# Neighbourhood attention block: four K window copies move from GpSimd to ScalarE

## The reference

```python
def _arsinh_norm(x, w, b):
    return w * jnp.arcsinh(x) + b
def _na2d(x, qkv_w, qkv_b, proj_w, proj_b, num_heads=8, k=3):
    qkv = x @ qkv_w + qkv_b
    q, kk, v = jnp.split(qkv, 3, axis=-1)
    ...
    nb_k = kk[:, ri, ci].reshape(B, H, W, k * k, num_heads, hd)   # the 3x3 neighbours, clipped at the edges
    nb_v = v[:, ri, ci].reshape(B, H, W, k * k, num_heads, hd)
    scores = jnp.einsum('bijnd,bijmnd->bijnm', q, nb_k)
    attn = jax.nn.softmax(scores, axis=-1)
    out = jnp.einsum('bijnm,bijmnd->bijnd', attn, nb_v).reshape(B, H, W, C)
    return out @ proj_w + proj_b
h1 = _arsinh_norm(h, n1_w, n1_b)
h = h + _na2d(h1, qkv_w, qkv_b, proj_w, proj_b)
h2 = _arsinh_norm(h, n2_w, n2_b)
ff = jax.nn.gelu(h2 @ mlp_w1 + mlp_b1, approximate=False) @ mlp_w2 + mlp_b2
return h + ff
```

## Time and profile before

| | |
|---|---|
| median of 3 runs | 4491.67 us (4490.61 to 4491.87) |
| the profiled execution | 4491.05 us, of which 4489.3 us are the span from the first to the last instruction |
| TensorE matmul, busy | 4311.2 us (96%) |
| VectorE, busy | 3710.5 us (83%) |
| ScalarE, busy | 3322.0 us (74%) |
| GpSimd, busy | 4023.6 us (90%) |
| mean granted TensorE clock | 0.991 of full |
| DMA, hardware queue | 591.32 MB, 50.6% of 16 engines |

### The profile page before, as it was taken

The page is one execution under the profiler, slowest core; times in us unless marked ns, Lnnn a source line. Parts: engine busy times, 40 slices in busy tenths (PEclk is TensorE's granted clock), DMA queues, the critical chain, the costliest instruction groups (busy, mean ns, idle before and its releaser), DMA issues.

```text
span 4489.3 us, 136686 instructions
## 1 busy us (share of the span) xinstructions
PE 4311.2 (96%) x53320; PEld 3075.6 (69%) x53320; DVE 3710.5 (83%) x7716; ACT 3322.0 (74%) x4865; POOL 4023.6 (90%) x4604
## 2 busy tenths in 40 slices
PE   3899999999999999999999999999999999999997
PEld 2577667667667667767767767766766766776775
DVE  4788888888888888888888888888888888888884
ACT  2677777777777777777777777777777777777774
POOL 1699999999999999999999999999999999999995
PEclk9899999999999999999999999999999999999998
DMA  3455555555555555555555555555555555555551
GB/s 77 127 137 140 137 136 141 138 136 141 136 136 140 136 137 136 140 138 137 138 138 138 138 139 137 138 139 135 141 136 136 141 135 137 139 138 137 138 133 50
DMA packets 593556, 600.06 MB, mean 134 GB/s; under 512 B 76559, under 2 KB 540561, under 8 KB 590353
## 3 DMA queue, kind: packets, MB, share of 16 engines
q1 hardware_dynamic: 592912, 591.32, 50.6%
HBM read 197.69 MB, written 135.40 MB: 74 GB/s over the span
## 4 chain that ended last, share of the span: by engine, by line
POOL 82%; issue 13%; PE 2%; DVE 1%; ACT 1%; SPq 1%; POOLq 0%; DMA 0%; DVEq 0%; ACTq 0%
POOL p_lo L1044 28%; POOL g_lo L1070 10%; POOL k_win L1087 10%; POOL b_hi L1059 7%; POOL a_lo L1052 6%; POOL b_lo L1061 6%; POOL g_hi L1068 6%; POOL a_hi L1050 3%; POOL k_win L1096 3%; POOL k_win L1104 2%; PE ps L378 2%; SPq L288 0%; POOLq L1042 0%; SPq L314 0%; DMA v_rows<-v_nat 0%
## 5 line engine op out<-in xcount | busy, mean ns | idle before, releaser
L1044 POOL TENSOR_TENSOR p_lo<-prob,p_hi 100x512 f16<-100x512 f32 x1024 | 1378.5, 1356 | 249.7 <-ACT p_hi L985 241.8
L984 ACT ACTIVATE prob<-ps 100x512 f32<-100x512 f32 x1024 | 612.8, 598 | 532.1 <-PE ps L378 530.6
L378 PEld LDWEIGHTS ps<-v_win,p_hi 100*128 100x128 f16 x8192 | 475.6, 98 | 247.6 <-issue 107.1
L843 DVE TENSOR_TENSOR o_norm<-ps,recip 64x128 f32<-64x128 f32 x2048 | 591.1, 289 | 49.4
L1070 POOL TENSOR_TENSOR g_lo<-g,g_hi 128x512 f16<-128x512 f32 x512 | 595.1, 1162 | 41.0
L985 ACT ACTIVATE p_hi<-ps 100x512 f16<-100x512 f32 x1024 | 616.4, 602 | 0.0
L812 DVE TENSOR_REDUCE ps<-ps 128x8 f32<-128x800 f32 x512 | 509.4, 995 | 85.0 <-PE ps L378 80.9
L378 PE MATMUL ps<-v_win,p_hi 100*128 100x65 f16 x8192 | 515.1, 193 | 60.5 <-POOL p_lo L1044 48.9
L378 PE MATMUL ps<-w_hi,g_hi 128*128 128x256 f16 x2048 | 560.7, 274 | 0.0
L378 PE MATMUL ps<-w_lo,g_hi 128*128 128x256 f16 x2048 | 560.5, 274 | 0.0
L378 PE MATMUL ps<-w_hi,g_lo 128*128 128x256 f16 x2048 | 560.5, 274 | 0.0
(11 more groups left out here) (103 smaller groups left out, 12106.9 us busy)
## 6 DMA issues: line engine op xcount, KB each, us to landing
keys<-k_win SPq DMA_DIRECT2D x1536, 100.0 KB, 2.2
v_win<-v_rows SPq DMA_DIRECT2D x1024, 101.6 KB
queries<-q_nat SPq DMA_DIRECT2D x1536, 64.0 KB
v_rows<-v_nat SPq DMA_DIRECT2D x256, 260.0 KB, 5.4
xin<-in_x_dram SPq DMA_DIRECT2D x128, 512.0 KB, 4.5
out_dram<-y SPq DMA_DIRECT2D x256, 256.0 KB, 3.1
queries<-in_query_mask_dram SPq DMA_DIRECT2D x128, 160.0 KB
keys<-in_mlp_w_dram SPq DMA_DIRECT2D x2, 512.0 KB, 6.3
```

Of the source, the lines that this page charges most:

```text
L378: return pe.matmul(o, a, b, start=start, stop=stop, skip_group_check=True)
L843: s = v.tensor_tensor(o_norm[r, c], av[r, :, HD * e:HD * e + HD], recip[c % 2][r].to_broadcast([NQ, PAIRS, HD]), ALU.mult)
L984: act.activation(prob[b][0:NK], ps[0:NK, B_ST + b, :], ACT.Exp, scale=INV * INV).then_inc(prob_ready, 1)
L1044: pool.tensor_tensor(p_lo[b][0:NK], prob[b][0:NK], p_hi[b][0:NK], ALU.subtract).then_inc(p_lo_ready, 1)
```

## The change

The four copies of `windows_main` leave GpSimd's k = 1 (lo = 0) and k = 2 (lo = 1) and become `Copy` activations on ScalarE, both pairs directly behind `k_high` in k = 0. The high pair waits for both high evictions and for the keys of the band that last used the buffer; the low pair waits for both `k_low` of VectorE. The signal `win_main` is now ScalarE's. `windows_bottom` and `windows_top` stay on GpSimd.

```diff
@@ -962,6 +963,21 @@
+            def windows_main(t, par, lo):
+
+                if lo == 0:
+                    act.wait_ge(k_hi_ready, signals(t, G, G))
+                    act.wait_ge(k_in[par], landed(t - 2, K_DMAS))
+                else:
+                    act.wait_ge(k_lo_ready, signals(t, G, G))
+                for g in range(G):
+                    a = k_nat[:, lo, g]
+                    rows = bass.AP(a.tensor, a.offset, [list(a.ap[0]), [TS, TILES], [PITCH, TS], [1, WIN]])
+                    to = k_win[par][:, lo, g].rearrange("p c (r j) -> p c r j", j=WIN)
+                    s = act.activation(to[:, :, 1:1 + TS], rows, ACT.Copy)
+                if lo == 1:
+                    s.then_inc(win_main, 1)
...
                     if k == 0 and pre:
                         k_high(t + 2, 0)
                         k_high(t + 2, 1)
+                        windows_main(t + 2, par, 0)
+                        windows_main(t + 2, par, 1)
@@ -1077,17 +1095,6 @@
-            def windows_main(t, par, lo):
-                if lo == 0:
-                    pool.wait_ge(k_lo_ready, signals(t, G, G))
-                    pool.wait_ge(k_in[par], landed(t - 2, K_DMAS))
-                for g in range(G):
-                    a = k_nat[:, lo, g]
-                    rows = bass.AP(a.tensor, a.offset, [list(a.ap[0]), [TS, TILES], [PITCH, TS], [1, WIN]])
-                    s = pool.tensor_copy(window_rows(par, lo, g)[:, :, 1:1 + TS], rows)
-                if lo == 1:
-                    s.then_inc(win_main, 1)
...
-                    if k == 1 and pre:
-                        windows_main(t + 2, par, 0)
                     if k == 2 and post:
                         b_parts(t - 1)
-                    if k == 2 and pre:
-                        windows_main(t + 2, par, 1)
```

More of the change, by code:

```diff
@@ L215, in build @@
             sem("pool_" + s) for s in ("a_hi", "a_lo", "b_hi", "b_lo", "g_hi", "g_lo", "p_lo"))
-        win_main, win_bottom, win_top = (sem("pool_win_" + s) for s in ("main", "bottom", "top"))
+        win_main = sem("act_win_main")
+        win_bottom, win_top = sem("pool_win_bottom"), sem("pool_win_top")
         block = ctx.enter_context(nc.Block())
```

## The result

| | before | after |
|---|---|---|
| median | 4490.61 us (5 runs, 4489.31 to 4491.87) | 4447.26 us (5 runs, 4444.31 to 4447.91) |
| ratio | | 0.9901, 95% interval 0.9887 to 0.9916 |
| the profiled execution | 4491.05 us, span 4489.3 | 4447.71 us, span 4445.9 |
| ScalarE busy | 3322.0 us (74%) | 3657.7 us (82%) |
| GpSimd busy | 4023.6 us (90%) | 3446.2 us (78%) |

What follows compares the result with a forecast made beforehand. It took two TensorE stalls on GpSimd in one stretch of the band, k = 3, as the bound. 4491 us less 125 bands x 0.28 = 35, plus 0.4 in the ramp, gave 4456 us, range 4394 to 4482.

Steps and rivals of the forecast that it cites:

- What bounds: One stretch, k = 3: TensorE loses 0.46 us to `p_lo` and 0.30 to `a_lo`, together 0.76 us a band.
- High copies worth 0: GpSimd, k = 1: removing the high copies gains 0, hidden by its wait for `p_hi` of tile 4.
- Low copies, 0.28 us a band by way of the order of `p_lo` and `sign1`: GpSimd, k = 2 to 3: `p_lo` of tile 7 goes ahead of `sign1`, `a_hi` starts earlier; 0.28 us a band.
- Elsewhere: K product to k = 2: path over TensorE, `p_hi`, `p_lo`, `b_hi`, `b_lo`, `sum1` unchanged, 0; ramp +0.4 us.
- ScalarE's copies: ScalarE, k = 0: four added copies at 0.72 us each fit before `prob` of tile 2; cost 0, bound 0.2 us a band.
- Nobody is shut out: Rival, k = 3: `a_hi` follows early, both TensorE stalls vanish, 0.76 us a band, 4396 us; chance 0.25 including half-way.
- No change: Rival, k = 3: `sign1` still starts before `p_lo` of tile 7, `a_lo` stall grows, 4491 us; chance 0.12.
- Slower: Rival, ScalarE before `prob` of tile 2: ten-element runs make copies slow; 4534 us at double price; chance 0.08.

Runs made afterwards that it cites:

- e1: Changed kernel with the two low copies back on GpSimd in k = 2, only the high ones on ScalarE: 4490.15 us, ratio 1.0001.
- e3: Changed kernel, but GpSimd's `p_lo` of tile 7 waits for VectorE's `o_low`, so `sign1` starts first: 4475.11 us, ratio 0.9966.
- e8: The changed kernel measured once more, nothing altered: 4443.10 us, ratio 0.9898.
- e5: Changed kernel with ScalarE's two low copies done a second time, a signal between the passes: 4554.14 us, ratio 1.0145.
- e6: Changed kernel, but TensorE's K product waits for the second `a_lo` only before its second channel group: 4433.25 us, ratio 0.9878.
- e9: Changed kernel with TensorE's `a_lo` wait split by channel group and VectorE's first-half `v_low` ahead of `sum2`: 4402.37 us, ratio 0.9805.
- e2: Changed kernel with the two high copies back on GpSimd in k = 1, only the low ones on ScalarE: 4443.86 us, ratio 0.9897.
- e4: Changed kernel, but VectorE does `sign1` ahead of `o_low` in k = 3: 4558.00 us, ratio 1.0150.
- e11: Kernel before, no copy moved, with TensorE's `a_lo` wait split and `v_low` ahead of `sum2`: 4495.63 us, ratio 1.0012.
- e12: Changed kernel with split `a_lo` wait, `v_low` ahead of `sum2`, and the two high copies back on GpSimd in k = 1: 4443.44 us, ratio 0.9894.

## Why the prediction was right

- **What bounds.** Right: one stretch, k = 3, with two stalls of TensorE. The wait for `p_lo` went, that for `a_lo` grew from 0.30 to 0.39 us; about 0.5 was told.
- **High copies worth 0.** Right by e1 (ratio 1.0001).
- **Low copies, 0.28 us a band by way of the order of `p_lo` and `sign1`.** Right in mechanism and size: `p_lo` ahead by 0.38 us, `sign1` 1.86 us, `a_hi` after 1.15 us of waiting, and the stretch from `sign1` to the K product shorter by 0.28 us; e3 turns that order by a wait and gives back 0.25 of it.
- **Elsewhere, "as now: 0".** Too small. The band lost 0.36 to 0.37 us, and of what is missing 0.07 lie between `sum2` and `sum1`. Two readings were wrong there. The row of 1.29 us is that of `sum2`, not of `sum1`, and it is not the time of an instruction that is first, which is 1.22: the `g_lo` before it held it. And the prediction led the path over `p_hi`, `p_lo`, `b_hi` and `b_lo` to `sum1`, where in both traces VectorE's own queue runs from `sum2` to `sum1` without a wait. With the 0.07 us the sum is 125 x 0.35 = 44 us. The result has 43 and e8, the same kernel, 46, so a time can't test the sum more finely.
- **ScalarE's copies.** 0.72 us told, 0.73 measured, so the short runs add nothing to the line drawn there; `prob` of tile 2 keeps 0.29 us of its wait. That ScalarE's operations go "by element count alone" is too strong: in the earlier trace rows 512 elements take 0.60 us as `prob` and 0.69 as `q_nat`. What a late `prob` costs was forecast too low: e5 was told at 0.57 us a band and costs 0.90.
- **Rivals.** *Nobody is shut out* (4396): the 1.86 us of `sign1` and e3 speak against it. Taking the `a_lo` stall away doesn't reach it (e6); e9 comes within 6 us of it, with `sign1` still shut out. *No change*: its deciding point was the right one, and e3 is that rival made to happen. *Slower*: not here, but e5 shows the place.

## What to carry to other kernels

When two engines shut each other out, the price of an instruction depends on its neighbour on the other engine: before crediting a shorter queue, look for who will be first after the shift, and then for the next pair, as e6 and e9 show. The 1.29 us of `sum2`, 0.07 us above the shortest of its kind, were such a neighbour here and not noise. Where an engine has no wait over a whole stretch, as VectorE here, each such overlap lengthens that stretch in full. And idle time by percentage says nothing of room: ScalarE at 82% had 0.3 us to spare at the one place that mattered.

## What the runs showed of the hardware

- A VectorE instruction of 1024 elements with two SBUF inputs takes 1.21 to 1.22 us alone. Shut out, it ends 1.07 to 1.08 us after GpSimd's instruction has ended (before, after, e1, e5, e6). So about the first 0.14 us of an overlap cost nothing (1.22 less 1.08): `sum2` started 0.12 us ahead of the end of `g_lo` in the changed kernel and in e2 and still took 1.22, and 0.21 us ahead in the kernel before and took 1.29. The other way round, GpSimd's `p_lo` ended about 1.0 us after `sign1` (before, e3, e4), its 1.16 us less a similar piece.
- This holds against `g_lo` and `p_lo` and also against GpSimd's float16 copies (e11, e12). The page "SBUF — State Buffer" of the Trainium skill (section "Who interferes with whom") says that the second fully blocks; the trace agrees but for those 0.14 us.
- A ScalarE copy of 128x640 float16 in runs of ten took 717 to 741 ns (512 of them), two of them 1.37 us. The page "ScalarE: Activation LUTs" of the Trainium skill (section "What ACT_TABLE_LOAD costs") gives an estimated 719 ns for 640 elements; the trace agrees, also for such short runs.
- `magnitude1`, a VectorE instruction with one SBUF input of 128x1024, takes 0.68 us at its shortest and 1.65 in the median (changed kernel); in the band shown it ends 0.55 us after the `p_lo` that ran beside it. That looks like the same exclusion, with one input instead of two, but no run here varies it, so it is not shown.
